# Lists of a routed layer built from digits of 64 and 17 instead of 128 and 9

## The reference, cut to what matters

```python
scores = sigmoid(x @ gate_weight.T)                 # 8240 x 16
top_s, top_idx = top_k(scores.T, 1030)              # each expert picks its tokens
routed[top_idx[e]] += top_s[e] * mlp_e(x[top_idx[e]])   # e = 0..15
out = routed + shared_mlp(x)                        # width 384
```

## Time and profile before

| | |
|---|---|
| Median of 3 runs | 4640.12 us (4629.51 to 4647.07) |
| The profiled execution | 4654.99 us |
| Its span | 4653.2 us |
| TensorE busy | 3991.2 us (86%) |
| VectorE busy | 2531.1 us (54%) |
| ScalarE busy | 1439.1 us (31%) |
| List loop | 684.7 to 924.4 us |

### The profile page before, as it was taken

One profiled execution on the slowest core, in us unless ns is written; L12 is line 12 of the kernel. 1 busy time (PEld: TensorE's weight loads), 2 busy tenths in 40 slices (PEclk: granted clock), 3 DMA queues, 4 the chain that ended last, 5 costly groups with the idle time before them and its releaser, 6 DMA issues. The chain is left out here.

```text
span 4653.2 us, 74405 instructions
## 1 busy us (share of the span) xinstructions
PE 3991.2 (86%) x24046; PEld 2485.3 (53%) x24046; DVE 2531.1 (54%) x4411; ACT 1439.1 (31%) x2890; POOL 1191.6 (26%) x1370
## 2 busy tenths in 40 slices
PE   8799777689999997664999999999957589898885
PEld 8688555557666665442233333333327566666664
DVE  1476369923222222786877777777824454444442
ACT  0122110011111111342577777777741111111110
POOL 0222010034444442464000000000013100177775
PEclk9899897789999998675899999999987699999998
DMA  6122111032333332345233224323239411377776
GB/s 207 49 65 54 40 38 28 25 75 59 61 61 69 70 63 45 105 128 134 42 56 61 47 47 66 50 47 51 48 81 239 106 30 47 88 165 159 162 160 148
DMA packets 335639, 381.02 MB, mean 82 GB/s; under 512 B 44708, under 2 KB 292035, under 8 KB 333823
## 3 DMA queue, kind: packets, MB, share of 16 engines
q1 hardware_dynamic: 255903, 289.46, 25.8%
q0 software_dynamic: 57856, 69.18, 8.7%
q10 hardware_dynamic: 21728, 20.14, 1.5%
HBM read 261.04 MB, written 123.33 MB: 83 GB/s over the span
## 5 line engine op out<-in xcount | busy, mean ns | idle before, releaser
L1931 DVE TENSOR_REDUCE at_mx<-psum 128x1 f32<-128x998 f32 (+1 forms) x768 | 886.4, 1192 | 264.1 <-PE psum L1756 263.5
L1886 ACT ACTIVATE at_p<-psum 128x512 f32<-128x512 f32 (+3 forms) x1536 | 851.5, 588 | 300.1 <-PE psum L1830 270.1
L1830 PE MATMUL psum<-at_q,at_k 99*128 99x512 bf16 (+3 forms) x1536 | 522.1, 383 | 20.3 <-issue 15.2
L1756 PE MATMUL psum<-at_k,at_q 96*128 96x512 bf16 (+3 forms) x1536 | 475.6, 392 | 66.7 <-DMA at_k<-qk_parts 29.3
L1816 PE MATMUL psum<-at_p,at_v 128*32 128x486 f32 (+3 forms) x3072 | 408.3, 604 | 1.0 <-ACT at_p L1886 0.7
L1830 PEld LDWEIGHTS psum<-at_q,at_k 99*128 99x128 bf16 (+1 forms) x1536 | 155.5, 102 | 426.6 <-ACT at_p L1886 273.3
L1173 DVE TENSOR_TENSOR ex_hT<-ex_silu,psum 128x384 f32<-128x384 f32 (+1 forms) x288 | 147.4, 512 | 416.2 <-ACT ex_silu L1142 271.0
L1142 ACT ACTIVATE ex_silu<-psum 128x384 f32<-128x384 f32 (+1 forms) x288 | 131.5, 457 | 776.5 <-PE psum L1086 646.2
L1736 POOL DMA_DIRECT2D o_parts<-at_o x24 | 12.9, 539 | 1247.9 <-DVE at_mx L1931 900.9
L1108 PE MATMUL psum<-ex_wd,ex_hT 128*128 128x192 f32 (+1 forms) x1728 | 291.5, 327 | 0.0
L1756 PEld LDWEIGHTS psum<-at_k,at_q 96*128 96x128 bf16 (+1 forms) x1536 | 152.4, 105 | 229.4 <-DVE at_mx L1931 64.0
(11 more groups left out here) (361 smaller groups left out, 6846.2 us busy)
## 6 DMA issues: line engine op xcount, KB each, us to landing
mx_wd<-in_e_dT SPq DMA_DIRECT2D x72, 288.0 KB, 3.9
qk_parts<-hd_parts SPq DMA_DIRECT2D x32, 579.4 KB, 3.8
at_k<-qk_parts SPq DMA_DIRECT2D x144, 128.8 KB
at_q<-qk_parts SPq DMA_DIRECT2D x144, 124.8 KB
tok_p<-in_x SPq DMA_DIRECT2D x12, 1176.0 KB
mx_wg<-in_e_gT SPq DMA_DIRECT2D x72, 192.0 KB, 2.4
mx_wu<-in_e_uT SPq DMA_DIRECT2D x72, 192.0 KB, 3.4
o_parts<-at_o POOLq DMA_DIRECT2D x24, 515.0 KB
```

The source lines that it names most:

```text
L1756: mm = pe.matmul(psum[0:ctx_rows[t], 3 + 2 * ((PRO + n) % 2) + k, 0:w], Q[v][0:R6, j * 1024 + 128 * t:j * 1024 + 128 * t + ctx_rows[t]], K ...
L1830: pe.matmul(psum[0:n, i % RING, 0:w], K[u][:, j, 128 * t:128 * t + n], Q[u][:, j * 1024 + at:j * 1024 + at + w], start=True, stop=True).th ...
L1886: act.activation(P[0:n, c % 2, j, 0:w], psum[0:n, i % RING, 0:w], ACT.Exp).then_inc(exp_ready, 1)
L1931: dve.tensor_reduce(mx[0:ctx_rows[t], j * CT + t:j * CT + t + 1], pair(n)[0:ctx_rows[t], 0:CTX], AX_X, ALU.max).then_inc(s_free, 1)
```

## The change

A place p in a list is now written as `hi` of 17 and `lo` of 64 (`LB`, `HB2`) instead of 9 and 128. `hot_lo` is 103 x 128 x 64 for a chunk, `hit` 103 x 128 x 17, and the weights of a list matmul are 34 columns, the moving side 64. The results of two experts (instead of four) lie side by side on the partitions, at 0 and 64, and eight groups of 64 columns along the bank.

`hot_lo` and `hot_hi` have two buffers each. `hot_lo` takes the same memory as before; `hot_hi` lies over five tiles of the search (`ones`, `above`, `equal`, `rank`, `take`, now one tile `wide`), which are dead by then. VectorE waits for the list matmuls of two chunks ago instead of those of the last. The loops go over pairs of chunks; on VectorE the first pair stands ahead of the loop.

`hit` is moved: from ahead of the first `hot_lo` to behind the fourth, right ahead of the `hot_hi` that read it. The unpacking into `ids` takes eight small instructions instead of four, and one memset clears the places that the shorter last column leaves. Core of the diff:

```diff
+    LB = 64
+    HB2 = -(-CAP // LB)
...
-        ones = sb("rt_ones", [128, SEQ])
-        above = sb("rt_above", [128, SEQ])
...
+        wide = sb("rt_wide", [128, 5, SEQ])
+        ones, above, equal, rank, take = (wide[:, k, :] for k in range(5))
...
-        hot_lo = sb("rt_hot_lo", [T, 128, 128], BF16)
-        hit = sb("rt_hit", [T, 128, ET], BF16)
-        hot_hi = sb("rt_hot_hi", [T, 128, 2 * ET], BF16)
+        hot_lo = sb("rt_hot_lo", [T, 2, 128, LB], BF16)
+        hit = sb("rt_hit", [T, 128, HB2], BF16)
+
+        hot_hi = wide[0:T, :, :].rearrange("p k n -> p (k n)").bitcast(BF16)[:, 0:2 * 128 * 2 * HB2] \
+            .rearrange("p (a n k) -> p a n k", a=2, n=128)
...
-            with pe.Fori(0, NC) as c:
-                j = c + LOOPS
-                shared_up(pe, j)
-                shared_down(pe, j)
-                pe.wait_ge(hot_ready, c + 1)
-                for b in range(B):
-                    for e in range(E0):
-                        q, g = e % 4, e // 4
-                        last = pe.matmul(psum[32 * q:32 * q + 2 * ET, 6, g * 128:(g + 1) * 128],
-                                         hot_hi[:, b * E0 + e, :], hot_lo[:, b * E0 + e, :],
...
+            with pe.Fori(0, NC // 2) as i:
+                for half in range(2):
+                    c = i * 2 + half
+                    shared_up(pe, c + LOOPS)
+                    shared_down(pe, c + LOOPS)
+                    pe.wait_ge(hot_ready, c + 1)
+                    for b in range(B):
+                        for e in range(E0):
+                            q, g = e % 2, e // 2
+                            last = pe.matmul(psum[LB * q:LB * q + 2 * HB2, 6, g * LB:(g + 1) * LB],
+                                             hot_hi[:, half, b * E0 + e, :], hot_lo[:, half, b * E0 + e, :],
...
+            dve.memset(ids[LB:128, :, ET - 1:ET], 0)
...
-                dve.tensor_tensor(hit[:], hi_c.unsqueeze(2).to_broadcast([T, 128, ET]),
-                                  iota_hi[:].unsqueeze(1).to_broadcast([T, 128, ET]), ALU.is_equal).then_inc(hit_ready, 1)
-
-                dve.wait_ge(hot_used, c)
-
+                if not first:
+                    dve.wait_ge(hot_used, c - 1)
                 for f in range(FC + 1):
...
                     if f < FC:
-                        shared_mult(dve, j, (f,))
+                        shared_mult(dve, c + LOOPS, (f,))
+                dve.tensor_tensor(hit[:], hi_c.unsqueeze(2).to_broadcast([T, 128, HB2]),
+                                  iota_hi[:].unsqueeze(1).to_broadcast([T, 128, HB2]), ALU.is_equal).then_inc(hit_ready, 1)
                 dve.wait_ge(hit_ready, c * 2 + 1)
...
+            for half in range(2):
+                list_chunk(half, half, True)
+            with dve.Fori(1, NC // 2) as i:
+                for half in range(2):
+                    list_chunk(i * 2 + half, half, False)
```

## The result

The median fell from 4643.1 us (4629.5 to 4647.1) to 4601.2 us (4599.1 to 4602.9): ratio 0.9912, 95% interval [0.9893, 0.9932]. That is 42 us, with 32 to 50 in the interval. The forecast was 4619, its range 4596 to 4641, which holds the time. But the gain is twice the one worked out. The time lies outside the narrow band of 4612 to 4627, to which 0.60 was given, and the change is a gain of over 0.5%, to which only 0.35 was given.

A forecast was written before the change was run, and what follows sets the result against it. VectorE bounded the list loop at 23.90 us a chunk, to become a 21.85 us ring with TensorE: 18.5 over nine, first chunk 6.6 gained, last 3.1, unpacking 0.5 and transposes 0.2 lost; 21.3 us, so 4619, range 4596 to 4641.

The forecast's parts named there:

- narrow band of 4612 to 4627: Forecast of the kernel's time, chance 0.60, from 1.7 to 3.1 us clock loss a chunk and lists of 2.1 to 2.6.
- The bound moves from VectorE's work to a ring: List loop: third multiply to `hot_ready` on VectorE, then TensorE's lists and `shared_up`, to the next third multiply; 21.85 us a chunk.
- The product with `row`: VectorE's product of `hit` with `row` in each chunk: 2176 elements between 1.11 and 1.25 us, taken as 1.19.
- The rival that this product loses its rate: Product with `row` at the two-operand rate, 2.42 us instead of 1.19; 11 to 20 us lost, about 4634; chance 0.08.
- The lists: TensorE's 128 list matmul pairs a chunk, 34 by 64 on two tiles: 2.2 us, between 2.12 and 4.6.
- The rival that two tiles don't overlap: Lists of 4.6 us at full clock, ring 24.25 us, kernel 4645 us; the slower side, chance 0.13.
- The clock: TensorE's 3.8 us pause drops its clock to half over lists and `shared_up`, losing 1.7 to 3.1 us a chunk, taken 2.1.
- The rival that the clock stays up: The 3.8 us pause leaves the clock at 1.00: ring 19.75 us, 42 us gained, 4598 us; chance 0.12.
- The moved `hit`: `hit` behind the fourth `hot_lo` puts its 2.45 us into the ring, costs some 1.8 us and lengthens TensorE's pause.
- The double buffers: The second pair of one-hot buffers only removes VectorE's 0.2 us wait for `hot_used` in a chunk.
- First chunk, last chunk, unpacking: Ends of the list loop and the code behind: 6.6 us gained, 3.1 lost, 0.5 lost plus 0.2 for transposes at half clock.
- same: Outcome class for the kernel's time, below the 0.5% that a measurement can tell; 0.39 + 0.08 + 0.10 and 0.01.

The follow-up runs named there:

- the kernels in which it never waits: Kernel after with `hit` ahead of the chunk's first `hot_lo`: 4557.05 us, ratio 0.9829; the same with one pair of one-hot buffers: 4567.2 us, ratio 0.9843.
- the two kernels with the same extra comparison: Kernel after plus a second, unread `hit` comparison: behind the fourth `hot_lo` 4639.6 us, ratio 1.0007; ahead of the first 4608.4 us, ratio 0.9942.
- the kernel with `hit` first: Kernel after with only the `hit` comparison put back ahead of its chunk's first `hot_lo`; digits and double buffers stay: 4557.05 us, ratio 0.9829.
- the kernel with one buffer: Kernel after with one pair of `hot_lo` and `hot_hi` buffers instead of two, `hit` still behind the fourth `hot_lo`: 4602.2 us, ratio 0.9925.
- the kernel with the filled pause: Kernel after plus fourteen matmuls of zeros, 512 columns each, while TensorE waits for `hot_ready`: 4589.8 us, ratio 0.9894.
- the digits alone: Against the kernel before, only digits 64 and 17; `hit` ahead of its chunk, one pair of one-hot buffers: 4567.2 us, ratio 0.9843.

## Why the prediction was right, and where its sizes were not

**The bound moves from VectorE's work to a ring**: right. The new digits took 6.4 us off VectorE's own work in a chunk (23.4, which is 23.9 less its waits of 0.2 and 0.28, to the 17.0 of the kernels in which it never waits); in the kernel after, a chunk's time fell by 3.4. The waits of both engines for one another show it, and so do the two kernels with the same extra comparison: 4.0 us a chunk inside the ring, under 0.1 outside.

**The ring's terms**, in the prediction's own order, from the chunk at 751.02. The lists at full clock are those of the same chunk in the kernel with `hit` first, 749.14 to 751.30; the loss to the clock is the rest of the 3.43 us between the same two starts here:

| term | predicted | measured |
|---|---|---|
| multiply, fourth `hot_lo`, `hit`, product with `tile0` | 0.50 + 2.20 + 2.45 + 2.34 | the same four |
| product with `row`, and TensorE's notice | 1.22 + 0.14 | 0.87 |
| lists at full clock | 2.2 | 2.16 |
| loss to the clock | 2.1 | 1.27 |
| `shared_up` | 8.57 | 8.57 |
| to the next third multiply | 0.13 | 0.10 |
| ring | 21.85 | 20.46 |

Two terms were too large, the clock by 0.8 us and the product with `row`, its notice included, by 0.5, and both in one direction. The 1.39 us in all make 12.5 us over nine chunks; in the first chunk the clock stayed up, 1.4 us more; and the nine chunks before were 23.86 us in the mean, not 23.90, 0.4 less. 18.5 + 12.5 + 1.4 - 0.4 = 32.0, against the 31.9 found.

**The product with `row`** failed at its bounds, 1.11 to 1.25 us: 0.813 is outside them. Both were drawn from the one row of 0.66 us for 1152 elements, with at most 0.15 us fixed. A line through the two sizes gives (0.813 - 0.660) / 1024 = 0.15 ns an element and 0.49 us beside. Both sizes are 128 pieces, of 9 elements and of 17, so the 0.49 can belong to the instruction or to its 128 pieces; no run tells which. A single row bounds a rate only if the part that doesn't grow is known, and 0.15 us was that of another form. The rival that this product loses its rate (0.08) fell.

**The lists** were sized right: 128 pairs on two tiles take 2.16 us to the next start at full clock where a turn of TensorE's loop follows (749.14 to 751.30), and 1.97 where none does (699.42 to 701.39). The 2.12 of the earlier trace rows had a turn behind every chunk. The four tiles before and the two after cost the same. The rival that two tiles don't overlap (0.13) fell: 15 to 16 ns a pair, as on four tiles. The Trainium skill's rule on weight loads (TensorE: Matmul & The Clock Gate, section LDWEIGHTS) gives 28 ns for 34 columns, and some 3.7 us, an estimate by that page, had the loads not hidden. The rows above show 1.97 and 2.16, so on two column tiles they hide.

**The clock** was right in kind and too large in size. The pause was forecast at 3.8 us and is 3.51. It falls, and costs the ring what runs low behind it. The step that failed is the length of the low stretch: 4.2 us (twice 2.1) was taken, between 3.3 and 6.14, and it is 3.41, so it ends with the lists, and `shared_up` keeps its full clock. The pairs of rows behind that choice showed how far such a stretch can differ; the first three chunks of the kernel with one buffer show that the length isn't a property of the pause. What was put at 2.1 us in each chunk was 0 in one and 1.4 in eight. The rival that the clock stays up (0.12, 4598 us) comes out near the truth in its total, for another reason: at full clock the ring is 19.0 to 19.2 us and not 19.75, as the first chunk and the kernel with the filled pause show, and in eight of nine chunks the clock fell after all.

**The moved `hit`** was priced at 1.8 us of the ring, beside a longer pause. Taken back, it gives 3.45 us: 2.2 for `hit`, after which VectorE's own 17.0 us bound the chunk, and 1.3 for the clock, which no longer falls once the pause is 1.05 us. The prediction named the longer pause and didn't price it; yet this was the largest thing found, 33 us in the profiled loops and 38 by the ratios, on top of the change's own 42.

**The double buffers** were put at 0.2 us of a chunk. Measured with `hit` behind: 20.48 against 20.46; with `hit` ahead: 17.01 both times. Nothing, then.

**First chunk, last chunk, unpacking**: 6.6, -2.1 and -0.7 us, against 6.6, -3.1 and -0.7. The lists of the last chunk are the row of 3.51 us at half clock. The eight small instructions of the unpacking take 1.23 us for 0.51.

**The chances.** With two sizes taken on the cautious side and the sum at 0.46%, the line at 0.5% was left to decide between "same" and "faster". The time fell between the forecast's band and the clock's rival, so the range held because it took in the rival's 4598 as well. Three of the signs named ahead were missed too: chunks of 20.5 us for 21 to 22.7, the product with `row`, and the low clock, which doesn't reach `shared_up`. And only the first multiply of a chunk waits for `shared_up`, not the second. The range was right to reach down to 4596; the weight of 0.58 on "same" was too much for a sum whose open terms could all but shrink.

## What to carry to other kernels

When a cheaper step moves the bound from one engine's work to two engines that wait for each other, write the ring down from start to start, and ask of every instruction between the release and the reader whether it could run elsewhere: the same 2.42 us comparison cost 4.0 us a chunk inside this ring and under 0.1 outside it. Count what the waiting engine loses behind the pause as well, here a clock that falls and comes back only under the next work. And an edit made of three parts should be measured in parts: the digits alone gave 1.6%, the double buffers nothing that can be told, and the move of `hit` took nearly half of it back (0.9% is left).

## What the runs showed of the chip

- A pause of TensorE of 3.51 us costs very different amounts. In the kernel after's first chunk the lists behind it ran at full clock (699.42, 2.04 us for 128 pairs), in all the steady ones at half (3.48), and in one execution of another kernel at least 8.5 us ran low behind the same pause. Pauses of 1.05 us left the clock at 1.00; one of 1.82 us, in the first chunk of the kernel with `hit` first, was followed by 3.3 us at 0.50.
- Pairs of 34 weight columns by 64 moving ones, on two column tiles, take 15 to 16 ns each at full clock (1.97 to 2.04 us for 128), as 18 by 128 on four tiles do (1.96).
- VectorE's product with a per-partition scalar (bf16) takes 0.81 us for 128 pieces of 17 elements and 0.66 for 128 of 9: the 1024 elements more cost 0.15 us. With two operands it is 1.35 us for 1152 elements, 2.28 for 2048, 2.42 for 2176 and 4.42 for 4096, some 1.04 ns for each element more.
- ScalarE takes 2.13 us for the same 2176 products that VectorE makes in 0.81:

```profile
744.37 2.13 ACT L806 ACTIVATE rt_wide<-rt_hit,rt_row 103x2176 bf16<-103x2176 bf16 x1
```
